# A fused two-layer transformer kernel: every block ends without GpSimd's drain, the experts' first two loads are issued before the last block change, forty matmuls stand ahead of it, and the last sequence's normalisation runs on VectorE

## The chip, the cores and the metric

The program runs on one core of one Trainium2 chip. The metric is the device time of one launch in microseconds: 2574.72 us before the change (median of 3 runs, 2572.01 to 2577.3). The engines are named as the profile names them: PE (TensorE), PEld (its weight loads), DVE (VectorE), ACT (ScalarE), POOL (GpSimd), SP (SyncE, here only an issuer of DMAs).

## The reference, cut to what matters

Inputs are 16 sequences of 512 tokens of 128 numbers. Two layers follow each other; in each an attention part and a feed-forward part read the same normalised input, and all is added to x.

```python
x = L0_attn_x                                   # (16, 512, 128)
xn = layernorm(x)
x = x + L0_attn(xn) + L0_ffn(xn)                # 16 heads with a decaying state; ternary MLP
xn = layernorm(x)
x = x + L1_attn(xn) + L1_ffn(xn)

def L1_ffn(src):                                # the part that the change touches
    attn = softmax(q @ k.T / sqrt(8)) @ v @ Wo + bo          # 16 heads of 8
    x = layernorm(src + attn) * ln1_g + ln1_b
    e = remainder(floor(x @ router_w + router_b), 4)         # one expert per token
    y = relu(x @ W1[e] + b1[e]) @ W2[e] + b2[e]
    return layernorm(x + y) * ln2_g + ln2_b
```

## The kernel before, in words

1. `layer0_sequences` (block at L225): layer 0, one sequence of 512 tokens after the other, software-pipelined. It ends at some 938 us.
2. `clear_released` (block at L2013): POOL alone clears semaphores.
3. The constants of layer 1 (block at L2110 in `layer1`): SP loads tables, the first `g1` (2 MB) and the split weights `f_hi`, `f_lo`; DVE and PE prepare small things.
4. `attention` (block at L1031): layer 1's attentions and its ternary MLP. The order is written out by hand (`attention_order`): 32 slots a round, in each a score product, an exponential and a row maximum of the 16-head softmax, and between them the other steps of up to eight stages, each on another sequence. Rounds run from -4 to 16, those from 2 to 11 in a hardware loop. Stage `C2` is the last: for a finished sequence it makes `mwo` (output projection and residual, DVE), statistics (DVE) and the root (POOL), `norm1` (DVE scales; POOL multiplies by the gain, adds the bias), `xr` (POOL: product with the router's weights), `keys` (DVE: which expert), `ahead`, `rank` and `slot` (where in the sorted table the token goes; two small products on PE), and `scatter`: four indirect DMAs issued by POOL (L1785), 128 rows of 257 numbers each, into `sorted_scratch` in device memory. After the last sequence DVE works out the plan `plan_i`: for each of 19 groups of 512 sorted rows the expert and the first row. POOL then waits until all scatters have landed (semaphore `sorted`), and the block ends.
5. `experts` (block at L1834): 19 tiles of 512 rows. SP reads the plan and loads for tile k the rows (`xt`, 5 buffers, 514 KB a tile, L1845) and the expert's weights (`wt`, 4 buffers, 834 KB, L1852). PE starts with four fp32 products of 128x512 that nobody reads (L1896, "warm-ups" below), transposes the rows (`turn`, L1869), ACT and DVE split them in two parts (`halve`, `rest`), PE does the first product (`first`, L1881 to L1883, three matmuls for each of 4 parts), ACT the relu (L1924), PE the second product (`second`, L1891, 16 matmuls of 128x128), DVE the second layernorm, POOL the root (`root`, L1991, L1994) and four indirect DMAs of the result (L2003). POOL's order is root(0), then for each k root(k+1) and the scatters of tile k. At the very end POOL waits until all of them have landed, and the program's last block ends.

Buffers: `prob` (the exponentials) is a tensor of the attention block, `g1_hi` one of the attention's weights and inputs; both are released before `experts` allocates `xt` and `wt`.

## Time and profile before

| what | us |
|---|---|
| median of 3 runs | 2574.72 |
| lowest, highest | 2572.01, 2577.3 |
| profiled execution, its own time | 2577.92 |
| its span, from the first to the last instruction | 2576.1 |
| PE / DVE / ACT / POOL busy in the span | 2364.5 / 1925.0 / 1340.2 / 594.0 |

The profiled execution took 2577.92 us, 1.82 more than its span, and lies 3.20 us above the median of the runs. Its mean granted TensorE clock was 0.957 of full speed (2.4 GHz).

The profile has several views. The timeline lists instructions in order of time, with the idle time before each and what ended it. The view by stretches gives busy time, granted clock and DMA traffic between two moments. The waits list who waited for whom, SP's queue among them. "SPq" is SP's queue, where an issued DMA is shown for the time that the issue took, not the transfer; "PEq" is a sequencer, which here stands for a barrier.

### The profile page before, as it was taken

Reading aid. Unit: us, or ns where it says so; the run is one execution under the profiler, and the core shown is the slowest. Engines: PE = TensorE matmul, PEld = TensorE weight load, DVE = VectorE, ACT = ScalarE, POOL = GpSimd, SP = SyncE. Lnnn points to the kernel's source line nnn. Section 1 sums busy time; section 2 is a strip of 40 time slices with the busy share of each in tenths; the row PEclk is TensorE's granted clock in tenths of the full one; section 3 lists DMA queues with packets and bytes.
Section 4 is the critical chain, followed back from the end, with each engine's and each line's share of the span. In section 5 each row is a group of like instructions: output and inputs, shape, how many; then the busy total and the mean of one; then the engine's idle time right before and its main releaser. Section 6 shows DMA issues by size and latency. Waiting matters only on the chain. (4 is left out here: it accounts for less than half of the span.)

```text
span 2576.1 us, 44713 instructions
## 1 busy us (share of the span) xinstructions
PE 2364.5 (92%) x14392; PEld 1644.7 (64%) x14392; DVE 1925.0 (75%) x3702; ACT 1340.2 (52%) x1927; POOL 594.0 (23%) x630
## 2 busy tenths in 40 slices
PE   8999999999999956899999999999999999888596
PEld 7788888888888845655555555555555555543495
DVE  6888888888888822767778777877778777873375
ACT  3454444444444412266666666666666666566242
POOL 1111122111121100112231222223131222213287
PEclk7999999999999978899999999999999999998798
DMA  5446322243222234233443334333443334211472
GB/s 181 129 136 174 86 80 80 85 129 100 84 80 80 78 113 136 90 79 102 137 133 94 89 115 143 100 88 108 133 132 96 87 115 112 68 53 42 158 236 94
DMA packets 195548, 280.28 MB, mean 109 GB/s; under 512 B 21672, under 2 KB 151161, under 8 KB 186880
## 3 DMA queue, kind: packets, MB, share of 16 engines
q1 hardware_dynamic: 189952, 266.47, 34.8%
q0 software_dynamic: 5504, 12.63, 1.4%
q8 instruction: 51, 0.84, 0.1%
q14 instruction: 41, 0.34, 0.0%
HBM read 148.65 MB, written 131.91 MB: 109 GB/s over the span
## 5 line engine op out<-in xcount | busy, mean ns | idle before, releaser
L1609 DVE TENSOR_REDUCE c_row_max<-b_psum 128x2 f32<-128x1024 f32 x512 | 624.0, 1219 | 217.0 <-PE b_psum L1308 210.8
L1452 ACT ACTIVATE c_prob<-b_psum 128x1024 f32<-128x1024 f32 x512 | 523.9, 1026 | 320.6 <-PE b_psum L1331 313.2
L1331 PE MATMUL b_psum<-c_cq,c_ck 25*128 25x512 f32 x1024 | 257.3, 501 | 39.3 <-ACT c_prob L1452 31.9
L1308 PE MATMUL b_psum<-c_bk,c_bq 24*128 24x512 f32 x1024 | 257.2, 501 | 29.8 <-DVE c_row_max L1609 22.8
L1342 PE MATMUL b_psum<-c_prob,c_v_aug 128*32 128x512 f32 x2048 | 280.3, 620 | 1.7 <-ACT c_ao_sb L1461 1.4
L1331 PEld LDWEIGHTS b_psum<-c_cq,c_ck 25*128 25x128 f32 x1024 | 95.3, 183 | 209.1 <-ACT c_prob L1452 111.7
L336 PE MATMUL a_psum<-a_yT_hi,a_w_hi 128*128 128x512 f32 x512 | 206.5, 403 | 9.9 <-issue 5.9
L336 PE MATMUL a_psum<-a_yT_hi,a_w_lo 128*128 128x512 f32 x512 | 204.0, 399 | 0.0
L336 PE MATMUL a_psum<-a_yT_lo,a_w_hi 128*128 128x512 f32 x512 | 203.5, 397 | 0.0
L465 ACT ACTIVATE a_g<-a_psum,a_cols 128x512 f32<-128x512 f32 x64 | 44.1, 690 | 237.3 <-PE a_psum L336 237.3
L557 DVE TENSOR_TENSOR_SCAN a_st_sb<-a_decay,a_kv_sb 128x512 f32<-128x512 f32 x128 | 158.0, 1234 | 4.4
L659 POOL TENSOR_TENSOR a_rs<-a_mv,a_eps 128x4 f32<-128x4 f32 x16 | 3.2, 203 | 630.8 <-DVE a_mv L580 630.8
L1308 PEld LDWEIGHTS b_psum<-c_bk,c_bq 24*128 24x128 f32 x1024 | 95.3, 184 | 81.5 <-DVE c_row_max L1609 61.1
L365 PEld LDWEIGHTS a_psum<-a_w_plain,a_outs 128*128 128x128 f32 x1024 | 134.2, 192 | 11.2
L365 PE MATMUL a_psum<-a_w_plain,a_outs 128*128 128x128 f32 x1024 | 134.8, 275 | 0.0
L1761 POOL TENSOR_TENSOR c_o_ms<-c_o_ms,b_minus_half 128x16 f32<-128x16 f32 x16 | 46.6, 2912 | 379.7 <-DVE c_o_ms L1592 379.7
L1196 PE MATMUL b_psum<-b_g_hi,b_f_hi 128*128 128x512 f32 x256 | 116.2, 454 | 16.4 <-DMA b_f_lo<-f_split_scratch 7.8
L554 DVE SCALAR_TENSOR_TENSOR a_kv_sb<-a_psum,a_bias,a_v_sb 128x512 f32<-128x512 f32 x128 | 95.5, 746 | 45.2 <-PE a_psum L336 26.2
L336 PEld LDWEIGHTS a_psum<-a_yT_hi,a_w_hi 128*128 128x128 f32 x512 | 97.5, 190 | 32.2 <-issue 10.7
L453 ACT ACTIVATE a_v_sb<-a_psum,a_bias 128x512 f32<-128x512 f32 x128 | 88.8, 694 | 49.4 <-PE a_psum L336 44.9
L336 PEld LDWEIGHTS a_psum<-a_yT_lo,a_w_hi 128*128 128x128 f32 x512 | 97.7, 191 | 22.9
L336 PEld LDWEIGHTS a_psum<-a_yT_hi,a_w_lo 128*128 128x128 f32 x512 | 97.6, 191 | 21.3
(303 smaller groups left out, 5334.7 us busy)
## 6 DMA issues: line engine op xcount, KB each, us to landing
sorted_scratch<-a_pad SPq DMA_DIRECT2D x16, 2184.5 KB, 14.7
g_scratch<-a_g_hi SPq DMA_DIRECT2D x16, 1024.0 KB, 4.0
g_scratch<-a_g_lo SPq DMA_DIRECT2D x16, 1024.0 KB, 7.1
b_g_hi<-g_scratch SPq DMA_DIRECT2D x16, 1024.0 KB, 6.7
b_g_lo<-g_scratch SPq DMA_DIRECT2D x16, 1024.0 KB, 8.8
stack_scratch<-c_qk_hi SPq DMA_DIRECT2D x256, 64.0 KB, 1.6
d_wt<-expert_scratch SPq DMA_DIRECT2D x19, 834.0 KB
c_bq<-stack_scratch SPq DMA_DIRECT2D x128, 96.0 KB
```

The lines of the kernel that those rows point to most:

```text
L336: mm = nc.tensor.matmul(out, a, c, start=(n == 0), stop=(n == last))
L365: mm = nc.tensor.matmul(tok[:, cut(t)], outs[:, i % OUTS, cut(t)], blk(w_plain, A_WO + i), start=(i == 0 and t == 0), stop=(i == FB0 - 1), ...
L453: nc.scalar.activation(v_sb[:, i % 2, :], bank(f"v{i}"), ACT.Identity, bias=bias[:, 4 * i:4 * i + 1]).then_inc(S["v"], 1)
L554: nc.vector.scalar_tensor_tensor(out=kv_sb[:, :], in0=bank(f"k{i}"), scalar=bias[:, 4 * i + 1:4 * i + 2], in1=v_sb[:, i % 2, :], op0=ALU.a ...
L557: nc.vector.tensor_tensor_scan(st_sb[:, :], decay[:, i:i + 1].to_broadcast([P, SEQ]), kv_sb[:, :], 0.0, ALU.mult, ALU.add).then_inc(S["sca ...
L1196: nc.tensor.matmul(bank(f"h2{c}"), hi, g1_hi[:, k, :], start=(k == 0), stop=False)
L1308: mm = nc.tensor.matmul(psum[:, max_bank(i, alone) + x, :], bq[r, j, cut(t)], bk[r, j, :], start=True, stop=True)
L1331: mm = nc.tensor.matmul(psum[:, score_bank(i, alone) + x, :], ck[r, j, cut(kb)], cq[r, j, :], start=True, stop=True)
L1342: mm = nc.tensor.matmul(psum[32 * g:32 * g + 32, value_bank(j, alone), :], v_aug[:, kb, HPG * j + g, :], prob[:, (2 * i + g // 2) % 4, g % ...
L1452: nc.scalar.activation(prob[:, i % 4, :, :], psum[:, at:at + 2, :], ACT.Exp, scale=DH1 ** -0.5).then_inc(S["exp"], 1)
L1609: nc.vector.tensor_reduce(row_max[:, t, at:at + 3:2], psum[:, bank0:bank0 + 2, :], AX.X, ALU.max).then_inc(S["row_max"], 1)
L1761: nc.gpsimd.tensor_tensor(o_ms[:, 2, :], o_ms[:, 1, :], minus_half[:, :], ALU.pow).then_inc(S["o_rms"], 1)
```

## The change

- All five blocks are opened with `no_gpsimd_drain=True`.
- At the end of SP's stream in the attention block SP waits for the last `pv` product and for the plan, loads the first expert's weights, waits for the scatters (`sorted`) and loads the first rows. Both loads stood at the head of the experts' block before. For this the first of the `wt` buffers lies in `g1_hi` and the first of the `xt` buffers in `prob`, which are now allocated ahead of both blocks (`first_tiles`).
- At the end of PE's stream in the attention block stand `TAIL_WARM` = 40 matmuls of 128x512 on `f_hi` that nobody reads.
- For the last sequence alone, the two steps of `norm1` and the step `xr` that POOL did are on DVE.

```diff
-        block = ctx.enter_context(nc.Block())
+        block = ctx.enter_context(nc.Block(no_gpsimd_drain=True))
...
+TAIL_WARM = 40
...
             run(sp, rounds)
+            first_x, first_w = first_tiles(prob, g1_hi)
             sp.wait_ge(S["r1_out"], 16 * BATCH)
+            sp.wait_ge(S["pv_done"], STEPS * BATCH)
+            sp.wait_ge(S["plan_i"], 1)
+            e = sp.value_load(plan_i[0:1, 0, 0:1], min_val=0, max_val=EXPERTS - 1)
+            sp.dma_start(first_w, d_table[bass.ds(e, 1), :, :].rearrange("e p w -> (e p) w")).then_inc(first_in[1], 16)
+            v = sp.value_load(plan_i[0:1, 1, 0:1], min_val=0, max_val=EXPERTS * CAP)
+            sp.wait_ge(S["sorted"], 16 * TILES * BATCH)
+            sp.dma_start(first_x, d_sorted[bass.ds(v, SEQ), :].rearrange("(t p) w -> p t w", p=P)).then_inc(first_in[0], 16)
...
             run(pe, rounds)
+            for n in range(TAIL_WARM):
+                nc.tensor.matmul(psum[:, PV, :], w_block(f_hi, n % HID), f_hi[:, 0:BANK], start=True, stop=True)
...
                     elif kind == "norm1":
                         norm_scale(stage, 1, x2, xf).then_inc(S["xh"], 1)
+                        if isinstance(base, int) and add == BATCH:
+                            dve.wait_ge(S["xh"], upto(stage, 1, 1))
+                            nc.vector.tensor_tensor(xf[:, :, :], xf[:, :, :], wide(R_G1), ALU.mult).then_inc(S["xg"], 1)
+                            dve.wait_ge(S["xg"], upto(stage, 1, 1))
+                            nc.vector.tensor_tensor(xf[:, :, :], xf[:, :, :], wide(R_B1), ALU.add).then_inc(S["xf"], 1)
+                            dve.wait_ge(S["xf"], upto(stage, 1, 1))
+                            nc.vector.tensor_tensor(xr[:, :, :], xf[:, :, :], wide(R_RW), ALU.mult).then_inc(S["xr"], 1)
...
+                    elif isinstance(base, int) and add == BATCH and kind in ("norm1", "xr"):
+                        continue
...
+def first_tiles(prob, g1_hi):
+
+    flat = prob[:, :, :, :].rearrange("p a b s -> p (a b s)")
+    weights = g1_hi[:, :, :].rearrange("p c s -> p (c s)").bitcast(F32)
+    return flat[:, 0:TILES * PAY].rearrange("p (t w) -> p t w", t=TILES), weights[:, 0:T_ROW]
...
-        xt = [sb(f"xt{n}", [P, TILES, PAY]) for n in range(XB)]
-        wt = [sb(f"wt{n}", [P, T_ROW]) for n in range(WB)]
+        first_x, first_w = first_tiles(prob, g1_hi)
+        xt = [first_x] + [sb(f"xt{n}", [P, TILES, PAY]) for n in range(1, XB)]
+        wt = [first_w] + [sb(f"wt{n}", [P, T_ROW]) for n in range(1, WB)]
...
-            load_rows(0)
-            load_expert(0)
             load_rows(1)
...
-    with nc.Block() as block:
+    with nc.Block(no_gpsimd_drain=True) as block:
```

How this moves instructions is shown at three places. The first is SP at the change from the attention block to the experts' block, before; `L886` and `L1836` are the end of one block and the start of the next.

```order
459 L1098 DMA c_xnb<-xnb_scratch 128x4x128
460 L1107 DMA c_pay<-r_scratch 128x4x128
461 L886 UNCONDITIONAL_BRANCH
462 L1836 UNCONDITIONAL_BRANCH
463 L1842 TENSOR_LOAD b_plan_i
464 L1842 ISA x2
465 L1845 ISA
466 L1845 DMA d_xt<-sorted_scratch 128x4x257
467 L1848 TENSOR_LOAD b_plan_i
468 L1848 ISA x2
469 L1852 ISA
470 L1852 DMA d_wt<-expert_scratch 128x1668
```

The same place after the change, where `L887` and `L1867` are the block's end and the next one's start, and `b_g_hi` and `b_prob` hold the first weights and rows:

```order
460 L1107 DMA c_pay<-r_scratch 128x4x128
461 L1145 TENSOR_LOAD b_plan_i
462 L1145 ISA x2
463 L1146 ISA
464 L1146 DMA b_g_hi<-expert_scratch 128x1668
465 L1147 TENSOR_LOAD b_plan_i
466 L1147 ISA x2
467 L1149 ISA
468 L1149 DMA b_prob<-sorted_scratch 128x4x257
469 L887 UNCONDITIONAL_BRANCH
470 L1867 UNCONDITIONAL_BRANCH
471 L1873 TENSOR_LOAD b_plan_i
```

Two reads of the plan and two DMAs moved from behind the block change to ahead of it, the weights now first.

The second place is DVE in the last sequence's stage `C2`, before:

```order
1091 L1505 TENSOR_SCALAR c_pay<-c_pay,c_mv,c_rs 128x128 x4
1092 L1633 TENSOR_TENSOR c_pay<-c_pay,c_step 128x4
1093 L1635 TENSOR_REDUCE c_keys<-c_xnb 128x4
1094 L1637 TENSOR_SCALAR c_keys<-c_keys,b_cols 128x4
1095 L1645 CAST c_keys_i<-c_keys 128x4
```

and after:

```order
1091 L1518 TENSOR_SCALAR c_pay<-c_pay,c_mv,c_rs 128x128 x4
1092 L1645 TENSOR_TENSOR c_pay<-c_pay,b_rows 128x4x128
1093 L1647 TENSOR_TENSOR c_pay<-c_pay,b_rows 128x4x128
1094 L1649 TENSOR_TENSOR c_xnb<-c_pay,b_rows 128x512
1095 L1653 TENSOR_TENSOR c_pay<-c_pay,c_step 128x4
1096 L1655 TENSOR_REDUCE c_keys<-c_xnb 128x4
```

Three products of 128x512 came in on DVE between the scaling and the keys; on POOL the same three are gone.

The third place is PE at the same block change, before:

```order
2466 L1296 MATMUL b_psum<-c_ahead,c_ones_row 128x20
2467 L1298 MATMUL b_psum<-c_mask,b_causal 128x16
2468 L886 UNCONDITIONAL_BRANCH
2469 L1862 UNCONDITIONAL_BRANCH
2470 L1896 MATMUL b_psum<-b_rows,b_ident 128x512 x4
2471 L1869 MATMUL b_psum<-b_ident,d_xt 128x128 x4
```

and after:

```order
2466 L1304 MATMUL b_psum<-c_ahead,c_ones_row 128x20
2467 L1306 MATMUL b_psum<-c_mask,b_causal 128x16
2468 L1376 MATMUL b_psum<-b_f_hi 128x512 x40
2469 L887 UNCONDITIONAL_BRANCH
2470 L1891 UNCONDITIONAL_BRANCH
2471 L1925 MATMUL b_psum<-b_rows,b_ident 128x512 x4
2472 L1898 MATMUL b_psum<-b_ident,b_prob 128x128 x4
```

Forty matmuls stand between the last product of `rank` and PE's arrival at the block's end.

## Rows read from the trace of the kernel before

**Rows 1.** The page: the chain that ended last, by engine, share of the span
```profile
issue 3%; POOL 3%; POOLq 0%; DVE 0%; DVEq 0%
```

**Rows 2.** Stretches: us, busy us (count) of five engines, clock, DMA share, GB/s
```profile
2403.60:2411.20 7.60, 0.00 (x0) 0.00 (x0) 0.00 (x0) 0.00 (x0) 0.00 (x0) 0.50 0.05 17
2568.20:2576.10 7.90, 0.00 (x0) 0.00 (x0) 0.00 (x0) 0.00 (x0) 0.00 (x0) 0.50 0.00 0
```

**Rows 3.** Timeline: the scatter before the last ones, and who waited for it
```profile
2380.20 0.96 POOL L1785 DMA_INDIRECT sorted_scratch<-c_pay,c_slot_i  x1 [0.30 <-issue]
...
2383.76 0.69 DVE L1624 TENSOR_TENSOR c_pay<-b_psum,c_xnb 128x512 f32<-128x512 f32 x1 [4.62 <-DMA sorted_scratch<-c_pay,c_slot_i]
```

**Rows 4.** SP's waits at the ends of blocks: us in total, times, longest
```profile
SPq L2013 <- PEq L2013: 0.6, 1, 0.6
SPq L2098 <- PEq L2098: 0.2, 1, 0.2
```

**Rows 5.** Timeline of the last sequence's `C2`, up to the last scatter
```profile
2387.21 1.12 DVE L1505 TENSOR_SCALAR c_pay<-c_pay,c_mv,c_rs 128x128 f32<-128x128 f32 x4 [1.44 <-POOL c_rs L1727]
...
2392.13 0.69 DVE L1635 TENSOR_REDUCE c_keys<-c_xnb 128x4 f32<-128x512 f32 x1 [3.73 <-POOL c_xnb L1775]
2392.86 0.23 DVE L1637 TENSOR_SCALAR c_keys<-c_keys,b_cols 128x4 f32<-128x4 f32 x1
...
2396.31 0.59 PE L1298 MATMUL b_psum<-c_mask,b_causal 128*128 128x16 f32 x2
2400.43 0.18 DVE L1713 CAST b_plan_i<-b_plan 128x38 int32<-128x38 f32 x1
...
2402.56 0.96 POOL L1785 DMA_INDIRECT sorted_scratch<-c_pay,c_slot_i  x1 [0.30 <-issue]
```

**Rows 6.** One DVE product of 128x512 from SBUF: ns min/median/max
```profile
L1972 DVE TENSOR_TENSOR d_first_acc<-d_xt,d_wt x19: 677/680/686, 2424.2 to 2549.4; 128x512 f32<-128x512 f32 x19
```

**Rows 7.** Timeline of the experts' start
```profile
2411.43 5.37 PE L1896 MATMUL b_psum<-b_rows,b_ident 128*128 128x512 f32 x8 [14.53 <-PEq L886]
2412.40 0.39 SPq L1845 DMA_DIRECT2D d_xt<-sorted_scratch  x1
...
2415.35 0.19 PEld L1896 LDWEIGHTS b_psum<-b_rows,b_ident 128*128 128x128 f32 x1 [0.24 <-issue]
2415.78 0.19 PEld L1896 LDWEIGHTS b_psum<-b_rows,b_ident 128*128 128x128 f32 x1 [0.24 <-issue]
2416.24 0.14 PEld L1869 LDWEIGHTS b_psum<-b_ident,d_xt 128*128 128x128 f32 x1 [0.27 <-DMA d_xt<-sorted_scratch]
...
2417.96 0.69 DVE L1934 TENSOR_TENSOR d_hT_lo<-b_psum,d_hT_hi 128x512 fp32r<-128x512 f32 x1 [17.34 <-ACT d_hT_hi L1915]
2420.17 0.50 PE L1881 MATMUL b_psum<-d_hT_hi,d_wt 128*128 128x512 f32 x1 [2.93 <-DMA d_wt<-expert_scratch]
```

**Rows 8.** Stretches: experts' start, the start of attention, the middle of the experts
```profile
2414.00:2416.00 2.00, 2.00 (x5) 0.91 (x4) 0.00 (x0) 0.00 (x0) 0.00 (x0) 0.79 1.02 344
2422.00:2424.00 2.00, 2.00 (x8) 1.71 (x8) 0.44 (x1) 1.16 (x2) 0.00 (x0) 0.50 1.11 426
954.00:960.00 6.00, 5.24 (x12) 3.80 (x12) 0.11 (x2) 0.00 (x0) 0.00 (x0) 0.50 1.02 388
2482.00:2523.00 41.00, 41.00 (x292) 37.51 (x291) 32.85 (x127) 20.63 (x32) 33.82 (x37) 1.00 0.68 228
```

**Rows 9.** Timeline, early in attention: one matmul, then five of the form added
```profile
1014.11 0.39 PE L1171 MATMUL b_psum<-c_xT_lo,b_w_hi 128*128 128x512 f32 x1
1014.35 1.32 PE L1185 MATMUL b_psum<-b_f_hi 128*128 128x512 f32 x5
```

**Rows 10.** Timeline: the second product of tiles 0 and 1, and POOL's last scatter
```profile
2426.99 3.74 PE L1891 MATMUL b_psum<-d_wt,d_hid 128*128 128x128 f32 x32
2433.80 3.74 PE L1891 MATMUL b_psum<-d_wt,d_hid 128*128 128x128 f32 x32
...
2567.21 0.98 POOL L2003 DMA_INDIRECT out<-d_out_sb,d_token  x1 [0.30 <-issue]
```

More of the change, by code:

```diff
@@ L884, in attention @@
               f_hi, f_lo, f_w3, f_scale, expert_id, place, place0, token0, plan, plan_i, d_x1, d_g1, d_full, d_stack, d_xnb, d_r1, d_sorted,
-              f_loaded, b_loaded, g1_hi, g1_lo, g1_in, d_b, d_cols):
+              f_loaded, b_loaded, g1_hi, g1_lo, g1_in, d_b, d_cols, prob, first_in, d_table):
     with ExitStack() as ctx:
@@ L948, in attention @@
         m_sb = sb("m_sb", [HEADS1 // 2, 2, SEQ], F32R)
-        prob = sb("prob", [P, 4, 2, SEQ])
         ao_sb = sb("ao_sb", [P, 2, SEQ])
@@ L1030, in attention @@
         r1_rows = d_r1.rearrange("a (t p) d -> a p t d", p=P)
-        block = ctx.enter_context(nc.Block())
+        block = ctx.enter_context(nc.Block(no_gpsimd_drain=True))
         def run(eng, rounds):
@@ L1490, in turn_on, with wide @@
                     dve.wait_ge(S[stage + "_filled"], upto(stage, len(uses[stage]), uses[stage].index(u) + 1))
+                def wide(row):
+                    return rows[:, row:row + 1, :].to_broadcast([P, TILES, P])
                 def norm_stats(stage, which, src):
@@ L1796, with experts @@
 T_ROW = T_B2 + P
-def experts(nc, psum, ident, rows, minus_half, eps, plan_i, d_sorted, d_table, d_out):
+def first_tiles(prob, g1_hi):
+    flat = prob[:, :, :, :].rearrange("p a b s -> p (a b s)")
+    weights = g1_hi[:, :, :].rearrange("p c s -> p (c s)").bitcast(F32)
+    return flat[:, 0:TILES * PAY].rearrange("p (t w) -> p t w", t=TILES), weights[:, 0:T_ROW]
+def experts(nc, psum, ident, rows, minus_half, eps, plan_i, d_sorted, d_table, d_out, prob, g1_hi, first_in):
     with ExitStack() as ctx:
@@ L1829, in experts @@
         Y, HT, RING = (0, 1), (6, 7), (2, 3, 4, 5)
-        sems(*(f"x_in{n}" for n in range(XB)), *(f"w_in{n}" for n in range(WB)))
+        S["x_in0"], S["w_in0"] = first_in
+        sems(*(f"x_in{n}" for n in range(1, XB)), *(f"w_in{n}" for n in range(1, WB)))
         sems("hT", "hT_hi", "hT_lo", "w1", "hid", "y", "acc0", "acc", "stats", "mv", "rs_step", "rs", "scaled", "token", "out", *(f"out_out{n}" for n in range(OB)))
@@ L1833, in experts @@
         out_rows = d_out.rearrange("a s d -> (a s) d")
-        block = ctx.enter_context(nc.Block())
+        block = ctx.enter_context(nc.Block(no_gpsimd_drain=True))
         @block.sync
@@ L2079, in layer1 @@
         psum = ctx.enter_context(nc.psum_tensor("b_psum", [P, 8, BANK], F32))
+        prob = sb("prob", [P, 4, 2, SEQ])
+        first_in = [ctx.enter_context(nc.semaphore(f"b_first_in{n}")) for n in range(2)]
         f_loaded = [ctx.enter_context(nc.semaphore(f"b_f_loaded{c}")) for c in range(HID)]
         b_loaded = ctx.enter_context(nc.semaphore("b_b_loaded"))
+        g1_hi = sb("g1_hi", [P, HID, SEQ], F32R)
         c2 = ctx.enter_context(ExitStack())
@@ L2086, in layer1 @@
         f_scale = c2.enter_context(nc.sbuf_tensor("b_f_scale", [P, HID], F32))
-        g1_hi = c2.enter_context(nc.sbuf_tensor("b_g1_hi", [P, HID, SEQ], F32R))
         g1_lo = c2.enter_context(nc.sbuf_tensor("b_g1_lo", [P, HID, SEQ], F32R))
@@ L2109, in layer1 @@
             fold_done = c1.enter_context(nc.semaphore("b_fold_done"))
-            block = c1.enter_context(nc.Block())
+            block = c1.enter_context(nc.Block(no_gpsimd_drain=True))
             @block.sync
@@ L2169, in layer1 @@
                   f_hi, f_lo, f_w3, f_scale, expert_id, place, place0, token0, plan, plan_i, d_x1, d_g1, d_full, d_stack, d_xnb, d_r1, d_sorted,
-                  f_loaded, b_loaded, g1_hi, g1_lo, g1_in, d_b, d_cols)
+                  f_loaded, b_loaded, g1_hi, g1_lo, g1_in, d_b, d_cols, prob, first_in, d_table)
         c2.close()
-        experts(nc, psum, ident, rows, minus_half, eps, plan_i, d_sorted, d_table, d_out)
+        experts(nc, psum, ident, rows, minus_half, eps, plan_i, d_sorted, d_table, d_out, prob, g1_hi, first_in)
 def kernel(**inputs):
```

## The prediction

> **What bounds the kernel now.** I read first the page's chain of waits, then the stretches around the two places that the change touches, then the timeline there. The chain that ended last [rows 1] is nearly all POOL and "issue", 3% each, and reaches back only into the experts' stage; it says that the end is set by the experts' tiles and, last of all, by POOL's scatters of the result. In the middle of that stage PE is busy for all of 41 us and POOL for 33.8 (its stretch from 2482 to 2523) [rows 8]: the tiles follow each other at PE's pace, so whatever moves the first tile moves the end by as much. The stretches then show two holes where no engine works at all, 7.60 us between attention and experts and 7.90 us at the very end [rows 2]. Both begin when POOL has issued its last indirect DMA. Everything before 2387 us (attention's loop, layer 0) is untouched but for two block ends, so the change is read in these two holes and in the chains just ahead of and behind the first.
>
> How long does a scatter take to land? For the sequence before the last the same four scatters ended their issue at 2380.20 + 0.96 = 2381.16, and DVE, which waited for them, started at 2383.76 [rows 3]: 2.6 us. In the first hole the last issue ends at 2402.56 + 0.96 = 2403.52 [rows 5], so the rows have landed at 2406.1, and the next block starts at 2411.2 to 2411.43 [rows 2, 7]. In the second it ends at 2568.19 [rows 10], landing at 2570.8, and the span ends at 2576.1. What is left is 5.1 and 5.3 us. A barrier to which POOL comes early, with nothing outstanding, costs SP 0.2 us of waiting at the end of the constants' block [rows 4]. I take 0.5 us for barrier and branch together (an estimate: that 0.2, and as much again for the branch and the first fetch); so POOL's drain after software DMAs is 4.6 to 4.8 us, twice.
>
> **The change part by part.**
>
> *The end of the program.* The drain goes, the landing and a barrier of 0.5 us stay: 2570.8 + 0.5 against 2576.1 is 4.8 us gained. Ends: nothing, if something else behind the block takes the same time, and 5.3, if the barrier is free. I take 4.8.
>
> *The block ends of layer 0, of the clearing and of the constants.* At the clearing's block POOL comes last, and SP waits 0.6 us there against 0.2 at the next block's end [rows 4]: 0.4 at most. I take 0.3. Behind the constants' block PE waits for weights in any case, so it gives nothing.
>
> *The last sequence's normalisation.* DVE ends its scaling at 2387.21 + 1.12 = 2388.33 and reduces the keys from 2392.13, having waited 3.73 us for POOL [rows 5]. On DVE a product of 128x512 out of SBUF takes 0.68 us [rows 6], and dependent DVE instructions follow each other after 0.04 (2392.13 + 0.69 to 2392.86, rows 5). Three are 2.16, and the addition of the token number, now behind them, 0.16: 2.32 against 3.80, 1.48 us gained. All behind it, the two small products on PE, the plan and the scatters, move with it: `rank` ends on PE at 2396.31 + 0.59 - 1.48 = 2395.4, the plan is ready at 2399.1, the last scatter is issued at 2402.0 and landed at 2404.6.
>
> *The early loads.* SP needs 1.2 us from the block's start to its first issue, for reading the plan (2411.2 to 2412.40, rows 7). So the weights are issued at 2399.1 + 1.2 = 2400.3. They are 834 KB; the queues move 344 to 426 GB/s when full [rows 8], so 2.0 to 2.4 us, and with some 2 us of fixed latency (the rows' 514 KB, 1.5 us of transfer, landed within 2416.24 - 2412.79 = 3.45, rows 7) they are there at 2404.9. The rows are issued at 2404.7, once SP sees the scatters landed, and are there at 2405.1 + 3.45 = 2408.5 at the latest. SP reaches the block's end at 2405.2.
>
> The weights now share the DMA engines with the scatters. Together they are 1.38 MB; at 344 GB/s from 2400.3 that is 4.0 us, and with 2 us of latency the scatters would land at 2406.3 instead of 2404.6. I keep 2404.6, nearer to rows 3, where the queues were also in use, and take 2406.3 as the other end; it reaches the block change at 2407.4, 0.1 us later than PE does below. The Trainium skill, "DMA: Bandwidth & Descriptors", section on queues, rings and completion order, speaks against the change here: a DMA's semaphore write lands only after every earlier write of its engine, across queues. By that rule the last scatters' signal cannot come before the weights are written, so the late end would be the right one, and the sum 0.1 us less; no run here shows it yet.
>
> *The forty matmuls.* They start at 2395.4. Five of this form took 1.32 us at the higher clock, and one matmul of 128x512 by itself is shown with 0.39 [rows 9], so they start (1.32 - 0.39) / 4 = 0.233 us apart. At 1.2 GHz twelve such took 5.24 us, 0.437 apart, and the clock read 0.50 through all of it (954 to 960) [rows 8]. Forty are 9.3 us at the one and 17.5 at the other. PE has been idle, so they start at 1.2 GHz. At the experts' start the clock was partly up in the stretch 2414 to 2416, 3 to 5 us after PE began, and fully by 2415.35, where the weight loads are 0.43 apart [rows 7, 8]. I take 4.4 us: ten slow ones and thirty fast ones, 4.4 + 7.0 = 11.4, ending at 2406.8. So PE, not POOL or SP, comes last to the barrier. The experts start on PE at 2407.3, 4.1 us earlier than 2411.43.
>
> *Behind the barrier.* The warm-ups took 4.8 us (2411.43 to 2415.78 + 0.43), eight passes partly at 1.2 GHz; with the clock up they are 8 x 0.43 = 3.4, 1.4 less. `turn(0)` starts at 2410.7; the rows have been there for 2 us, so the warm-ups are what is late next. From `turn(0)` to the first product it was 3.93 us, of which PE waited 2.93 for the weights [rows 7]; now DVE's part is last, 2417.96 + 0.69 + 0.1 - 2416.24 = 2.5, 1.4 less. The first product starts at 2413.2 instead of 2420.17: 6.9 us gained, the 1.48 among it. Then before had a stretch at half clock, 2422 to 2424 [rows 8], behind PE's wait for the weights; 2 us at half speed are 1 us lost. PE still pauses 2.5 us there, so I take 0.5 of it back (ends 0 and 1.0). The later loads are issued 4 us earlier with 1.4 MB less ahead of them, so they don't become the bound. From the second product of tile 1 (2433.80) to POOL's last scatter it is 133.4 us [rows 10], taken as unchanged.
>
> **The sum** against the profiled execution of 2577.92 us: 6.9 + 0.5 + 4.8 + 0.3 = 12.5, so 2565.4. That execution lies 3.2 us above the median of the runs; on the median the forecast is 2574.72 - 12.5 = 2562.2.
>
> **The rivals.**
>
> *The end's drain is not saved.* Whatever closes the program may wait for the same thing. For it: the hole at the end has no instruction in it, so the profile doesn't say what it is. Against it: 5.1 and 5.3 us at two places that have only the block's end in common. Gain 7.7, 2567.0.
>
> *The forty matmuls stay at 1.2 GHz.* For it: rows 8, 12 matmuls and no rise. Against: rows 7, the rise within 5 us. PE ends at 2412.9, the experts start at 2413.4, the warm-ups take 4.8 and the split 2.5: first product at 2420.7, 0.5 later than before. With end and clearing the gain is 4.6, 2570.1: a wait for PE has taken the place of the one for POOL.
>
> *The flag leaves POOL's drain in.* Then landing at 2404.6, drain and barrier 5.1, experts at 2409.7, first product at 2415.6: 4.6 + 0.5 = 5.1 gained, 2569.6.
>
> *Slower: the clock falls in the experts' stage.* The row 2422 to 2424 shows that it does fall there after a pause of 2.9 us, and PE sets the pace. A tile at half clock costs a further 6.8 us (2433.80 - 2426.99 is one tile's period, rows 10). From the second such tile the gain of 12.5 is gone; with three the time is 2562.2 + 20.4 = 2582.6. Against it: the clock reads 1.00 from 2482 to 2523, and PE now has fewer pauses than before, not more.
>
> **How the numbers follow.** Forecast 76%, the end's drain not saved 10%, matmuls slow 7%, flag without effect 4%, slower 3%. The forecast's own ends: the clock's rise and the pause behind it (±1.5), the barrier (±1) and the spread of a median of a few runs (±2). The range 2557.5 to 2568 holds the forecast's ends and the first rival, and leaves out the other three and some tails. 0.2% is 5.1 us, about what a measurement of this kernel can tell from no change: faster by more than that, below 2569.6, has the forecast, the first rival and half of the next two, 0.91; within it 0.06; slower 0.03.
>
> **What would show it.** In the changed kernel's profile: the hole at the end is 3 us and not 7.9 (else the first rival). Between POOL's last scatter of attention and PE's first fp32 warm-up lie some 5 us, and PE's forty matmuls end last before it, after POOL's wait for the landing; if they run 17 us, the second rival. DVE's three products take 2.2 us and POOL has none there. `turn(0)` follows the warm-ups without a wait for rows, and the first product comes 2.5 us behind it with no wait for weights. The second product of tile 1 to POOL's last scatter is again 133 us. The forecast is wrong if that distance grows, or if the time before 2387 us changes by more than 1 us: then the moved buffers do something that I have not priced.

## The result and the profile after

The changed kernel takes 2558.68 us (median of 8 runs, 2551.12 to 2566.35) where the kernel before takes 2576.01 (8 runs beside it, 2564.48 to 2585.34): ratio 0.994, 95% interval 0.9921 to 0.9959. In two later series of 12 and 9 runs the same kernel had 0.9958 (0.9933 to 0.9983) and 0.9953 (0.9933 to 0.9973). The three ratios together say some 12 to 13 us; one alone is good to 5 or 6. The forecast was 2562.2 us, a gain of 12.5.

The profiled execution took 2566.35 us, with a span of 2564.6. The two holes of [rows 2] are now these (stretch, us, busy time of PE, PEld, DVE, ACT and POOL, clock, DMA share, GB/s):

```profile
2403.71:2409.15 5.44, 4.03 (x18) 3.01 (x17) 0.00 (x0) 0.00 (x0) 0.00 (x1) 1.00 0.45 185
2562.92:2564.60 1.68, 0.00 (x0) 0.00 (x0) 0.00 (x0) 0.00 (x0) 0.00 (x0) 0.50 0.01 0
```

Each runs from the end of POOL's last scatter issue to PE's first warm-up, or to the end. At the end of the program 7.9 us became 1.7. Between attention and experts it is 5.4 us instead of 7.9, and it is no longer empty: PE is busy with the forty matmuls and the DMA queues move weights.

The traces also hold every DMA packet, and they show how much of the old holes was landing. In the kernel before, the scatters' last packet ends 1.1 us behind the last issue's end in the first hole and 0.8 us behind it in the second. After that nothing moves; the DMA view of 2404.7 to 2411.4 says, and that of 2569.0 to 2576.1 says the same:

```profile
DMA packets 0, 0.00 MB, mean 0 GB/s; under 512 B 0, under 2 KB 0, under 8 KB 0
```

From the last packet to the end of the program it is 7.2 us with the drain (two traces) and 0.9 us without it (eleven traces).

Just ahead of it, on DVE, the answer to [rows 5]:

```profile
2389.00 1.12 DVE L1518 TENSOR_SCALAR c_pay<-c_pay,c_mv,c_rs 128x128 f32<-128x128 f32 x4 [1.44 <-POOL c_rs L1747]
2390.15 0.69 DVE L1645 TENSOR_TENSOR c_pay<-c_pay,b_rows 128x512 f32<-128x512 f32 x1
2390.88 0.69 DVE L1647 TENSOR_TENSOR c_pay<-c_pay,b_rows 128x512 f32<-128x512 f32 x1
2391.61 0.69 DVE L1649 TENSOR_TENSOR c_xnb<-c_pay,b_rows 128x512 f32<-128x512 f32 x1
2392.22 0.16 DVE L1653 TENSOR_TENSOR c_pay<-c_pay,c_step 128x4 f32<-128x4 f32 x1
2392.33 0.69 DVE L1655 TENSOR_REDUCE c_keys<-c_xnb 128x4 f32<-128x512 f32 x1
```

Nothing waits any more between the scaling and the reduction: 3.33 us from start to start, where [rows 5] have 4.92.

The start of the experts, the answer to [rows 7, 10]:

```profile
2396.95 10.80 PE L1376 MATMUL b_psum<-b_f_hi 128*128 128x512 f32 x40
...
2400.64 0.18 DVE L1733 CAST b_plan_i<-b_plan 128x38 int32<-128x38 f32 x1
2402.28 0.01 SPq L1146 DMA_DIRECT2D b_g_hi<-expert_scratch  x1
2402.75 0.96 POOL L1807 DMA_INDIRECT sorted_scratch<-c_pay,c_slot_i  x1 [0.31 <-issue]
2408.26 0.39 SPq L1149 DMA_DIRECT2D b_prob<-sorted_scratch  x1
2409.18 3.67 PE L1925 MATMUL b_psum<-b_rows,b_ident 128*128 128x512 f32 x8 [1.44 <-PEq L887]
...
2412.69 0.60 PE L1898 MATMUL b_psum<-b_ident,b_prob 128*128 128x128 f32 x4
2414.02 0.69 DVE L1963 TENSOR_TENSOR d_hT_lo<-b_psum,d_hT_hi 128x512 fp32r<-128x512 f32 x1 [13.19 <-ACT d_hT_hi L1944]
2414.85 0.47 PE L1910 MATMUL b_psum<-d_hT_hi,b_g_hi 128*128 128x512 f32 x1 [1.57 <-DVE d_hT_lo L1963]
```

Tile 0's weights are read into `g1_hi`'s memory (shown as `b_g_hi`) and its rows into `prob`'s. SP issues the rows 4.55 us behind the end of the last scatter's issue (2403.71), PE starts its warm-ups 0.9 us later, and the first product comes 11.14 us behind that issue, where it was 16.65. The half-clock stretch of [rows 8] is gone:

```profile
2422.00:2424.00 2.00, 2.00 (x21) 2.00 (x20) 0.58 (x1) 0.00 (x0) 0.00 (x0) 1.00 0.97 342
```

One thing is not as forecast: everything up to `C2` is 1.8 us later in this execution (2389.00 against 2387.21 for the scaling), although attention's loop is the same. So I compare distances, not times. "The last x2 addition" is the first DVE step of the last sequence's `C2` (`c_pay<-b_psum,c_xnb`, 2383.76 in [rows 3], 2385.55 here). From it to the second product of tile 1 it was 50.04 us (2433.80 - 2383.76, rows 3 and 10) and is 42.09 (2427.64 - 2385.55); from there to POOL's last scatter 133.41 and 134.30; from that issue's end to the span's end 7.91 and 1.68. Together 13.3 us, less the 1.8 is the 11.5 between the spans.

### The profile page after: what moved, and what is told of

Its sections match the earlier page's. It is cut to its first block and busy times, and to the rows that moved or that the text cites. A ratio compares the mean times of both kernels' runs of the same rounds, so it can differ in the third digit from the quotient of the medians.

```text
span 2564.6 us, 44808 instructions
## 1 busy us (share of the span) xinstructions
PE 2372.4 (93%) x14432; PEld 1650.5 (64%) x14432; DVE 1928.3 (75%) x3705; ACT 1339.1 (52%) x1927; POOL 591.8 (23%) x627
## 5 line engine op out<-in xcount | busy, mean ns | idle before, releaser
L1462 ACT ACTIVATE b_prob<-b_psum 128x1024 f32<-128x1024 f32 x512 | 523.9, 1026 | 324.5 <-PE b_psum L1339 310.7
L1350 PE MATMUL b_psum<-b_prob,c_v_aug 128*32 128x512 f32 x2048 | 281.2, 622 | 1.7 <-ACT c_ao_sb L1471 1.4
L365 PEld LDWEIGHTS a_psum<-a_w_plain,a_outs 128*128 128x128 f32 x1024 | 133.9, 191 | 11.8
```

Of the source, the lines that this page charges most:

```text
L365: mm = nc.tensor.matmul(tok[:, cut(t)], outs[:, i % OUTS, cut(t)], blk(w_plain, A_WO + i), start=(i == 0 and t == 0), stop=(i == FB0 - 1), ...
L1350: mm = nc.tensor.matmul(psum[32 * g:32 * g + 32, value_bank(j, alone), :], v_aug[:, kb, HPG * j + g, :], prob[:, (2 * i + g // 2) % 4, g % ...
L1462: nc.scalar.activation(prob[:, i % 4, :, :], psum[:, at:at + 2, :], ACT.Exp, scale=DH1 ** -0.5).then_inc(S["exp"], 1)
```

## The experiments

Eleven runs, ten of them timed several times, "moved buffers" once. The theory: the change is separate things that add up, and most of the gain is the drain, paid twice. The rivals: the flag does all of it, or only its end does, or the early start carries it. Each edit is made to before or to the changed kernel, as said. Figures from the eleven traces and the first two: "Rows", "PE" and "product" are us from the end of the last sorted-row scatter's issue to tile 0's rows issued, to PE's first fp32 warm-up and to the first product; "to tile 1" is from the last x2 addition to tile 1's second product; "end" from the last result scatter's issue to the span's end; "slow" counts tiles more than 7 us apart. A time written as +11.0 is counted from the same point as the first three columns.

| kernel | rows | PE | product | to tile 1 | end | slow | ratio (95%) |
|---|---|---|---|---|---|---|---|
| before | 8.88 | 7.91 | 16.65 | 50.04 | 7.91 | 0 | 1 |
| end flag only | 8.43 | 7.47 | 15.75 | 48.45 | 1.69 | 0 | 0.9977 (0.9954-1.0001) |
| flags only | 3.25 | 2.28 | 11.00 | 43.21 | 1.66 | 1 | 0.9948 (0.9925-0.9971) |
| flags, moved buffers | 3.33 | 2.37 | 10.97 | 43.14 | 1.65 | 0 | one run, 2571.4 us, before beside it 2570.97 |
| flags, norm on DVE | 3.19 | 2.23 | 10.60 | 41.94 | 1.65 | 4 | 0.9942 (0.992-0.9964) |
| changed, drains back | 4.38 | 9.98 | 17.38 | 47.95 | 7.96 | 5 | 0.9992 (0.9972-1.0012) |
| changed, no forty | 4.38 | 5.30 | 13.22 | 44.17 | 1.67 | 0 | 0.998 (0.9953-1.0007) |
| changed | 4.55 | 5.47 | 11.14 | 42.09 | 1.68 | 2 | 0.994 (0.9921-0.9959) |
| changed, 2nd | 4.40 | 5.50 | 11.18 | 42.12 | 1.65 | 0 | 0.9958 (0.9933-0.9983) |
| changed, 3rd | 4.32 | 5.51 | 11.19 | 42.13 | 1.69 | 0 | 0.9953 (0.9933-0.9973) |
| weights last | 2.11 | 4.43 | 10.11 | 41.06 | 1.66 | 12 | 0.9929 (0.9903-0.9955) |
| short start | 2.10 | 3.56 | 8.11 | 39.05 | 1.63 | 0 | 0.9937 (0.991-0.9964) |
| short start, 2nd | 1.99 | 3.45 | 7.82 | 38.75 | 1.69 | 5 | 0.9934 (0.9909-0.9959) |

**Flags only.** The kernel before with one edit, five times:

```
-block = ctx.enter_context(nc.Block())
+block = ctx.enter_context(nc.Block(no_gpsimd_drain=True))
```

> The kernel before with the flag alone, on all five blocks: no early loads, no forty matmuls, norm1 and xr of the last sequence on POOL. Theory (the change is three separate things): the experts' block ends 6.2 us earlier (last scatter's issue to the end of the program 1.7 us instead of 7.9), the attention block's end hands over about 4.1 us earlier (from the last sorted-row scatter's issue end to the first fp32 warm-up about 3.8 us instead of 7.9), and the ends of layer 0's and the constants' blocks give under 0.4 us. The warm-ups still run at the low clock (4.8 us for eight passes) and turn(0) to the first product stays 3.9 us. Sum -10.3 us, ratio 0.996. Rival 1, the flag is the whole change: ratio 0.994, and the other three parts hid behind something. Rival 2, only the end of the program is worth something because PE waits for SP's loads at the attention block's end anyway: -6.2 us, ratio 0.9976.

The hole and what follows it:

```profile
2387.57:2389.80 2.23, 0.00 (x0) 0.00 (x0) 0.00 (x0) 0.00 (x0) 0.00 (x0) 0.50 0.16 59
```

```profile
2389.85 6.71 PE L1896 MATMUL b_psum<-b_rows,b_ident 128*128 128x512 f32 x8 [8.91 <-PEq L886]
2390.82 0.39 SPq L1845 DMA_DIRECT2D d_xt<-sorted_scratch  x1
...
2398.57 0.47 PE L1881 MATMUL b_psum<-d_hT_hi,d_wt 128*128 128x512 f32 x1 [1.57 <-DVE d_hT_lo L1934]
```

The handover shrinks from 7.91 to 2.28 us, more than the 4.1 expected, and the first product comes at +11.0: as early as in the whole change. The slow warm-ups (6.71 us, the clock 0.50 up to 2396) cost little here: in a like kernel below PE finished them earlier and then waited for tile 0's weights until +10.6, so 0.4 us at most. The timing, 13.5 us by medians, is between the theory (0.996) and rival 1 (0.994), and no less than the average of the changed kernel's three ratios, 0.995: by time, the flag alone can't be told from the whole change. By the traces the change is 1.1 us earlier at tile 1 (42.1 against 43.2). Rival 2, that PE would wait for SP's loads just as long, falls.

**End flag only.** The same edit on the experts' block alone.

> The kernel before with the flag on the experts' block alone. The prediction's step said 4.8 us (bounds 0 to 5.3) for the end of the program; the trace after shows 1.7 us from the last scatter's issue to the end where it was 7.9, which would be 6.2 us. Theory: -6.2 us, ratio 0.9976, hole at the end 1.7 us in the profile, everything before the last scatter as before. Rival 1 (the step as predicted, the scatters' landing still waited for): -4.8 us, ratio 0.9981, hole about 3 us. Rival 2 (what left the span is paid after the last instruction): the span is 6.2 us shorter but the time is not, ratio 1.000, and time minus span grows from 1.8 to 8 us.

```profile
2560.73 0.98 POOL L2003 DMA_INDIRECT out<-d_out_sb,d_token  x1 [0.30 <-issue]
```

The issue ends at 2561.71 and the span at 2563.4: 1.69 us. The execution took 2565.15 us, so time minus span is 1.8 us as before; the drain has not moved behind the last instruction. The 6.2 us are shown by the hole; the ratio agrees, though its interval just reaches 1. Up to tile 1 this kernel is the kernel before, and it took 48.45 us where the other execution took 50.04: executions differ by 1.6 us there, in the handover (0.4), behind it up to the first product (0.5) and in tile 0 (0.7). In tile 0 the half-clock stretch of [rows 8] is missing:

```profile
2414.00:2421.00 7.00, 6.32 (x33) 4.78 (x34) 1.29 (x2) 4.98 (x8) 0.00 (x0) 1.00 1.03 390
```

It is missing, too, in the three other kernels with tile 0's loads in the old place: of five traces with that start only before's has it.

**The changed kernel with the drains back.**

```
-block = ctx.enter_context(nc.Block(no_gpsimd_drain=True))
+block = ctx.enter_context(nc.Block())
```

> The changed kernel with the flag taken off all five blocks again: early loads, forty matmuls and norm1/xr on VectorE stay. Theory (parts add up, about 10.3 of the 15.5 us are the drains'): -1.5 us of norm1 and xr, the clock stays high into the experts (warm-ups 3.7 instead of 4.8 to 5.4 us, no half-clock stretch 0.9 us), turn(0) to the first product 2.2 to 2.5 instead of 3.9 us; together about -4.5 us, ratio 0.998. The drain again ends about 4 us after the scatters' landing, so the warm-ups start near 2412. Rival 1 (overlap): the early loads only matter because the drain is gone, and with the drain the clock falls again in its idle time after the forty matmuls (they end near 2407.7): warm-ups at 1.2 GHz, -2 us, ratio 0.999. Rival 2 (the drain lasts longer with the weights' transfer under way): more than 5 us between the rows' issue and the warm-ups, ratio 1.000.

```profile
2407.07 0.39 SPq L1149 DMA_DIRECT2D b_prob<-sorted_scratch  x1
2412.67 5.41 PE L1925 MATMUL b_psum<-b_rows,b_ident 128*128 128x512 f32 x8 [5.88 <-PEq L887]
```

```profile
2406.00:2408.00 2.00, 0.78 (x4) 0.32 (x2) 0.00 (x0) 0.00 (x0) 0.00 (x0) 1.00 0.02 6
2408.00:2410.00 2.00, 0.00 (x0) 0.00 (x0) 0.00 (x0) 0.00 (x0) 0.00 (x0) 0.83 0.87 238
2410.00:2412.00 2.00, 0.00 (x0) 0.00 (x0) 0.00 (x0) 0.00 (x0) 0.00 (x0) 0.50 0.08 25
```

Here 5.6 us pass from the rows' issue to PE's first warm-up, so rival 2 is right in size. It is not right in cause: from the scatters' last packet (+3.6) to PE it is 6.4 us, and 6.8 and 6.4 in the two kernels with the drain and no weights' transfer (last packet +1.1). The drain is no longer than there; it starts later. The clock falls to 0.50 while PE waits, as rival 1 said, and the warm-ups take 5.4 us. The first product is later than before's (17.38 against 16.65). Up to tile 1 this kernel is 2.1 us below before, but only 0.5 below "end flag only", less than the 1.6 that the norm on DVE gives by itself. With a drain in the way, the early start is wasted. Together with "flags only" this adds up within the intervals: 0.9948 and 0.9992 make 0.994.

**Weights last.** In the changed kernel SP issues tile 0's weights behind its rows:

```
-sp.dma_start(first_w, ...).then_inc(first_in[1], 16)
 v = sp.value_load(plan_i[0:1, 1, 0:1], ...)
 sp.wait_ge(S["sorted"], 16 * TILES * BATCH)
 sp.dma_start(first_x, ...).then_inc(first_in[0], 16)
+sp.dma_start(first_w, ...).then_inc(first_in[1], 16)
```

> The changed kernel with tile 0's weights issued after tile 0's rows, so behind the wait for the last scatters. Theory (the weights' transfer holds up the last scatters' completion): SP's wait for the scatters ends 2.6 us after the last scatter's issue instead of 4.55 us, rows issued near 2406.3 instead of 2408.3; then PE's fortieth matmul (end 2407.75) is the last to reach the barrier, so the warm-ups start only 0.4 to 0.6 us earlier (about 1.0 us behind PE's last); weights land before the first product. Ratio to the kernel before 0.9938, 0.5 us less than after. Rival 1 (the 4.55 us are the scatters' own): rows issue at the same time, ratio as after, 0.994. Rival 2 (the weights are now what the first product waits for): weights land about 4 us behind their issue together with rows, first product at about 2415.5, 0.5 us later than after, ratio 0.9942.

```profile
2399.00 0.96 POOL L1807 DMA_INDIRECT sorted_scratch<-c_pay,c_slot_i  x1 [0.31 <-issue]
2402.07 0.39 SPq L1148 DMA_DIRECT2D b_prob<-sorted_scratch  x1
2402.64 0.36 SPq L1149 DMA_DIRECT2D b_g_hi<-expert_scratch  x1
2404.39 3.67 PE L1925 MATMUL b_psum<-b_rows,b_ident 128*128 128x512 f32 x8 [0.42 <-PEq L887]
```

The theory holds: with no other transfer under way SP sees the scatters landed after 2.1 us, with the weights ahead of them after 4.3 to 4.55. The DMA packets show where the time goes. From 0.68 us before the last scatter's issue end to 1.72 behind it, the changed kernel (first line) moves weights alone, and this one (second line) the last two scatters (queue: packets, MB, share of the 16 DMA engines; q1 is SP's, q0 POOL's):

```profile
q1 hardware_dynamic: 92, 0.61, 77.0%
q0 software_dynamic: 95, 0.26, 30.2%
```

The third scatter's data start at -0.7 here and at +1.7 there, just behind most of the weights' 128 packets, which run from -0.8 to +2.9; the last packet of all four scatters ends at +1.1 here and at +3.4 there. So the scatters' own data are late by the 2.3 us.

PE's fortieth matmul is now the last to the barrier, and the first product is 1.0 us earlier. The Trainium skill, "DMA: Bandwidth & Descriptors", section on queues, rings and completion order, says that a DMA's semaphore write lands only after every earlier write of its engine, across queues; nothing here speaks against it, but it isn't what cost the 2.3 us, since the data before that write were late by as much.

This execution lost its gain again between tile 1 and the end (138.80 instead of 133.4 us): twelve tiles follow each other at 7.13 us (the first) and 7.30 to 7.46 instead of 6.80. Two of them:

```profile
2444.17 3.84 PE L1920 MATMUL b_psum<-b_g_hi,d_hid 128*128 128x128 f32 x32 [0.31 <-ACT d_hid L1953]
2451.54 3.84 PE L1920 MATMUL b_psum<-d_wt,d_hid 128*128 128x128 f32 x32 [0.33 <-ACT d_hid L1953]
```

PE waits 0.3 us for ACT there, and in [rows 10] not at all. The middle of the stage, where [rows 8] have PE busy for all of 41 us:

```profile
2482.00:2523.00 41.00, 39.46 (x272) 35.07 (x272) 29.82 (x114) 16.16 (x28) 29.88 (x34) 1.00 0.67 205
```

The granted clock is 1.00 here as there. The changed kernel's first profile has two such tiles, 0.9 us.

**Moved buffers.** Before with the flags and with `prob` and `g1_hi` allocated ahead, tile 0's loads where they were.

> The flag on all five blocks and the moved buffers (prob and g1_hi allocated ahead, tile 0, 5, ... rows in prob's and tile 0, 4, ... weights in g1_hi's memory), but tile 0's loads where they were, no forty matmuls, norm1 and xr on POOL. In the three profiles of kernels with the moved buffers the distance between second products of neighbouring tiles is 7.11 to 7.13 us from tile 2 to 3 and 7.36 to 7.39 us for the next one to twelve, then 6.80 us again; in the three without them it is 6.80 us but for two tiles of one. Theory A (the place of the buffers makes the slow tiles): 7.1 us from tile 2 to 3 and about 7.38 after it here as well, 0.9 us or more lost between tile 1's second product and the last scatter (133.4 us in before). Theory B (the early start makes them, by the earlier loads or by a TensorE that comes in at the high clock): all tiles 6.80 us but for a stray one, 133.4 to 133.7 us. Elsewhere as the kernel with the flag alone: first product 11.0 us behind the last sorted-row scatter's issue end, end hole 1.7 us.

Every tile up to the last two is 6.78 to 6.82 us apart, and it is 133.41 us to the last scatter. One trace without slow tiles settles little, since the second and third of the changed kernel have none either. Both theories fall with "flags, norm on DVE", which has neither moved buffers nor the early start and shows 7.15, 7.35, 7.39 and 7.18. Whether either makes slow tiles more frequent is open: two of the four traces without moved buffers have them, and four of the nine with them.

**No forty matmuls.** The changed kernel with `TAIL_WARM = 0`.

> The changed kernel without the forty matmuls. Theory (they hold the clock and nothing else): SP's wait for the scatters ends as in after (4.55 us behind the last scatter's issue end), the eight warm-up passes start at about +5.4 us at 1.2 GHz and take 5.4 instead of 3.7 us, turn(0) and tile 0's first half run at the low clock in part; the first product comes at about +13.5 us instead of +11.1, and tile 0 takes some 0.8 us more. Ratio to the kernel before 0.9952, about 3 us more than after. Rival 1 (the forty matmuls aren't needed, the warm-ups alone raise the clock behind a wait that hides them): first product within 0.5 us of after's, ratio 0.994. Rival 2 (a colder start keeps the slow tiles away): no tile over 6.85 us, and 0.9 us of the loss comes back, ratio 0.9949.

```profile
2400.58 5.92 PE L1925 MATMUL b_psum<-b_rows,b_ident 128*128 128x512 f32 x8 [11.89 <-PEq L887]
...
2408.50 0.47 PE L1910 MATMUL b_psum<-d_hT_hi,b_g_hi 128*128 128x512 f32 x1 [1.57 <-DVE d_hT_lo L1963]
```

The warm-ups run at the low clock and the first product is 2.0 to 2.1 us later, tile 0 no slower: given the early loads, the forty matmuls are worth 2.0 us to tile 1 (44.17 against 42.1). The ratio, 0.998, says more (0.9958 beside it), within its interval. No tile is slow here, as rival 2 said, but seven of the 13 traces have none.

**The changed kernel again, twice.**

> The changed kernel once more, with a profile of its own. Theory (the later times in the first profile before the changed place were the execution's own): the stretch from the first product of the second layer to the last sequence's x2 addition differs from 1433.4 us by some us either way, as it does among kernels that are alike there (1423.4 to 1433.5 us), while the stretches around the change repeat within 0.2 us: rows issued 4.55 us, warm-ups 5.47 us, first product 11.14 us behind the last sorted-row scatter's issue end, end hole 1.68 us. Ratio 0.9935 to 0.9945. Rival (the moved buffers cost time in the second layer): 1433 us again and more. The slow tiles (7.1 us from tile 2 to 3, then 7.36) show again if they belong to this kernel and not to one execution.

> The changed kernel a third time, beside the two others. Theory: first product at +11.1 to +11.2 us, end hole 1.65 us, x2 addition to the end 177.9 us plus 0.55 us for each slow tile; ratio 0.9945. Slow tiles showed in one of its two profiles: either result says only how often they come.

The places around the change repeat within 0.25 us (the table's rows). The stretch of attention does not: from the second layer's first product to the last x2 addition it is 1443.2 and 1427.2 us, after 1433.4 in the first profile. Over all 13 traces it lies between 1422.0 and 1443.2; the average is 1427.0 for the four without the moved buffers and 1431.7 for the nine with them. The spread among kernels of one kind (1422.0 to 1443.2 within the nine) is larger than that difference, so a cost of the moved buffers in attention is neither shown nor excluded.

**A shorter start.** Weights last, 28 matmuls, two fp32 warm-ups:

```
-TAIL_WARM = 40
+TAIL_WARM = 28
...
-for n in range(4):
+for n in range(2):
     nc.tensor.matmul(psum[:, Y[1], :], ident[:, :], rows[:, 0:TILES, :]...
```

> A version meant to be faster: tile 0's weights behind tile 0's rows, 28 matmuls instead of 40 at the attention block's end, two fp32 warm-ups (four passes) instead of four. Theory (warm-ups and PE's tail are what is late once the scatters' completion is not held up): behind the last sorted-row scatter's issue end the rows are issued at +2.1, the matmuls end at +1.2, warm-ups start at +2.4 and take 1.9 us, turn(0) at about +4.8 when the rows are there, first product at +7.1 us (after 11.14, weights last 10.11). 4.0 us less than after, ratio 0.9925 or less. Rival 1 (the first tile's data is late): turn(0) at +5.5 or weights landing at +8, first product at +8.5, 2.6 us less than after. Rival 2 (the clock falls in the shorter cover): first half of tile 0 at 1.2 GHz, +10 or more. Rival 3 (the gain is lost in slow tiles, of which the kernel with the weights last had twelve): up to 5 us between tile 1 and the last scatter, ratio as after's or above.

> The version with tile 0's weights behind its rows, 28 matmuls and two fp32 warm-ups once more, on the same chip as after. Theory: first product at +8.1 us, x2 addition to the end 174.8 us, 3.1 us less than after (177.9); ratio to the kernel before 0.993. Rival (the 3.1 us were that execution's): first product anywhere else than at +8.0 to +8.3. If slow tiles (over 7 us) show up, each costs about 0.55 us on top in either kernel.

```profile
2382.29 9.47 PE L1376 MATMUL b_psum<-b_f_hi 128*128 128x512 f32 x28
2392.61 1.95 PE L1925 MATMUL b_psum<-b_rows,b_ident 128*128 128x512 f32 x4 [0.85 <-PEq L887]
2394.93 0.66 PE L1898 MATMUL b_psum<-b_ident,b_prob 128*128 128x128 f32 x4 [0.37 <-DMA b_prob<-sorted_scratch]
2397.16 0.47 PE L1910 MATMUL b_psum<-d_hT_hi,b_g_hi 128*128 128x512 f32 x1 [1.57 <-DVE d_hT_lo L1963]
```

The first product comes at +8.11 and +7.82, 3.1 and 3.4 us earlier than in the changed kernel; `turn(0)` now waits for the rows, so this is near what the loads allow. The theory's +7.1 was too early: the 28 matmuls end at +1.2 in the second execution but at +2.7 in the first (7.99 and 9.47 us), PE is not through the barrier before +3.45 in either, and `turn(0)` comes 3.6 to 3.8 us behind the rows' issue, with the weights moving beside them. In time it is 0.9937 and 0.9934, each some 0.002 below the changed kernel in the same series. That agrees with the 3 us (0.001), but no interval tells them apart, and the second execution gave 3.1 us back with five slow tiles (136.25 us from tile 1 to the last scatter, 133.13 in the first).

**Flags and the norm, nothing else.**

> The kernel before with two parts of the change: the flag on all five blocks, and norm1 and xr of the last sequence on VectorE. No moved buffers, no early loads, no forty matmuls. Theory (early loads and forty matmuls together are worth nothing as they stand: the loads hold up the scatters' completion by about 2.3 us, and the flag alone had its first product at +11.0 us as after has): first product 11.0 us behind the last sorted-row scatter's issue end, x2 addition to that issue end 18.15 instead of 19.76 us, x2 addition to the end of the program 177.6 to 178 us where after has 177.9 without slow tiles; ratio to the kernel before 0.9942, as after's. Rival 1 (the early loads and forty matmuls carry some of the gain): 2 us or more behind after, ratio 0.9955 or above. Rival 2 (norm1 on VectorE only pays together with the early loads): 179.2 us as the flag alone.

```profile
2389.28 5.80 PE L1908 MATMUL b_psum<-b_rows,b_ident 128*128 128x512 f32 x8 [8.83 <-PEq L886]
...
2397.65 0.50 PE L1893 MATMUL b_psum<-d_hT_hi,d_wt 128*128 128x512 f32 x1 [2.13 <-DMA d_wt<-expert_scratch]
```

41.94 us to tile 1, where the whole change needs 42.1, and a ratio of 0.9942: the theory holds. Tile 0's early loads and the forty matmuls are worth nothing together in the form that they have; in the form of "a shorter start" the traces show 3 us for them. From the x2 addition to the end this trace has 179.89 us, but 1.9 of it are the slow tiles (135.32 instead of 133.4).

## Why the prediction held

*The total* was right: 12.5 us forecast, and three measured ratios that average to 0.995, 12.8 us. The place of the gain was right too: two holes behind POOL's last scatters, a drain in each. The closeness of the total is partly luck. The first series alone has 0.994, 15.5 us. The traces from the last x2 addition to the end give 13.3, 14.4 and 13.8 us against before's trace, and 1.4 us less each when before is taken as "end flag only" plus its 6.2 us of drain; and errors of both signs cancel below. The steps, by what the traces give:

*The end of the program:* forecast 4.8 us (at most 5.3), measured 6.2, beyond the upper end. The mis-sized term is the landing: I kept 2.6 us of it, from [rows 3], and 0.5 for the barrier. The whole of it, landing and barrier, is 1.63 to 1.69 us in all eleven traces with the flag there, 0.8 of it up to the last packet. The 2.6 were DVE's wait, not the landing: in [rows 3] too, the scatter's last packet ends 1.1 us behind the issue, and in the changed kernel the same wait is 2.17. What held DVE for the rest stays open. So the drain costs 6.2 us at the end, not 4.8, and the rival that it is not saved falls. Between the blocks it was read too small by the same error: the flag alone takes 5.2 to 5.7 us out of the handover, not 4.6 to 4.8.

*Layer 0, clearing, constants:* forecast 0.3, measured nothing. From `x_scratch`'s issue to `b_cols`' it is 3.38 us, after 3.39, and the waits of [rows 4] are

```profile
SPq L2042 <- PEq L2042: 0.5, 1, 0.5
SPq L2129 <- PEq L2129: 0.2, 1, 0.2
```

POOL has no transfer of its own under way there: the first packet of its queue moves at 1264 us.

*The normalisation on DVE:* forecast 1.48, measured 1.60 in the first profile (19.76 to 18.16 us from the x2 addition to the last scatter's issue end) and 1.60 to 1.62 in the others.

*Early loads:* the weights are issued 1.1 to 1.5 us behind the plan (forecast 1.2), and SP sees the scatters at +4.3 to +4.55. In the forecast's time that is its late end, 2406.3, and not the 2404.6 that I took; "weights last" shows the weights to be the reason. What the packets show there is data that wait behind the weights, not a signal held back. The late end cost next to nothing, as said there, as PE came about as late.

*Forty matmuls:* forecast to take 11.4 us and end at +4.8, measured at +4.0 in the first profile and +5.1 in the two others. PE's first warm-up was forecast at +5.3 and came at +5.5. "PE comes last to the barrier" holds in two of three traces (PE waits 0.4 us there). In the first, SP was last, held by the scatters: PE waited 1.44 us at the barrier and SP 0.2.

*Behind the barrier:* warm-ups 3.67 us (forecast 3.4), `turn(0)` to the first product 2.2 (2.5). The first product was forecast at +11.2 and came at +11.14 to +11.19. For the half-clock stretch I took 0.5, at most 1.0. Tile 0 is 0.8 us shorter than in before's trace, but the stretch was that execution's and not the old start's: "end flag only", at full clock, is 0.15 slower than the changed kernel there, and "flags only" 0.3 faster. The term rested on a row that one execution in five shows.

*133.4 us unchanged:* 134.30, 133.16 and 133.73 in the changed kernel's three traces. By the prediction's own words it is wrong if that distance grows; it grew by 0.9 us in the first, with two slow tiles, and not in the two others. Slow tiles came in six of 13 traces, with and without the moved buffers and the early loads.

*The rivals:* the forty matmuls took 10.8 to 11.8 us, not 17; the flag alone cuts the handover from 7.9 to 2.3 us, so it does take the drain out; and the clock stayed at 1.00 through the experts' tiles, the slow ones too.

The rise of 1.8 us ahead of 2387 was named as a sign of something not priced. The repeats show that this stretch wanders by more than that, so the condition was too tight to tell anything.

What the forecast lacked is the other side: I priced the loads and the matmuls as what brings the 6.9 us, and never asked what the flag alone would give. It gives the first product at +11.0 by itself.

## What to carry to other kernels

A block that ended with GpSimd's indirect DMAs cost 5 to 6 us here for the drain on top of their landing and the barrier; look for holes in which no engine works behind the last such issue, and take them away first. A large prefetch that is issued ahead of the last small transfers goes first on the DMA engines, and here delayed their data by 2.3 us: put it behind the wait that everyone needs. Price each part of a joint change alone as well: here the early loads and the forty matmuls between them gave nothing that the flag alone did not.

## What was not expected of the hardware

- The drain lasts much longer than the landing that it follows: 7.9 us behind the last scatter's issue against 1.7 with the flag at the end of the program, and 7.5 to 7.9 against 2.2 to 2.4 between attention and experts. Counted from the last packet it is 7.2 us at the end and 6.4 to 6.8 between the blocks, also where a weights' transfer made that packet 2.5 us later. At block ends ahead of which POOL had issued no DMA it costs nothing that shows (3.39 against 3.38 us).
- Two scatters of 132 KB each, whose packets would have started 0.1 and 1.4 us behind the first packet of an 834 KB load, had to wait until most of that load was through: in five traces their data started 2.4 to 2.7 and 1.9 to 2.3 us later than without it.
- The experts' tiles have a second pace, 7.1 to 7.5 us instead of 6.80, for one to twelve tiles and beginning with the step from tile 2 to 3 in five of six traces. PE then waits 0.2 to 0.4 us for ACT at most second products, at a granted clock of 1.00. ACT's first relu behind a second product's start comes at 4.9 to 5.3 us in slow tiles and at 4.47 in the settled pace (some tiles of 6.80 us have it late too), though the matmul that it waits for is at most 0.1 us later; it starts 0.05 us behind the start or the end of DVE's addition from PSUM (`d_acc`). What starts and ends this stays open: neither the moved buffers nor the early start is needed for it, and nothing else was tried.
- Identical code in the constants' block took 9.8 to 12.9 us from its first to the next block's first load, where single loads took SP up to 2.08 us to issue instead of 0.43.
